# Four reorderings in a fused attention and ternary-FFN kernel: row statistics stored ahead of token transposes, two weight turns and a column sum moved, output-weight splits gathered in one place

## The reference

```python
xn = (x - mean(x)) / sqrt(var(x) + 1e-5)
q, k, v = rope(xn @ Wq.T), rope(xn @ Wk.T), xn @ Wv.T
s = softmax(causal(q @ k.T / sqrt(32))) @ v @ Wo.T
def bitlinear(x, w):                    # w: sign(round(w / (mean|w| + eps))) * mean|w|
    return absmax_clip(layer_norm(x)) @ ternary(w).T
g = silu(bitlinear(gelu(bitlinear(xn, w_fc)), w_proj))   # 512 -> 2048 -> 512
out = x + s * g
```

## Time and profile before

| | |
|---|---|
| runs | 1117.98, 1117.86, 1116.13 us; median 1117.86 |
| the profiled execution | 1117.98 us; its span in the trace 1116.3 us |
| mean granted TensorE clock | 0.997 |
| PE busy (matmul) | 1087.4 us, 97% |
| DVE, ACT, POOL busy | 865.5 us (78%), 771.7 us (69%), 519.8 us (47%) |
| PE's waits from 290 us to the end | none listed |

### The profile page before, as it was taken

The page is one execution under the profiler, slowest core; times in us unless marked ns, Lnnn a source line. Parts: engine busy times, 40 slices in busy tenths (PEclk is TensorE's granted clock), DMA queues, the critical chain, the costliest instruction groups (busy, mean ns, idle before and its releaser), DMA issues.

```text
span 1116.3 us, 19950 instructions
## 1 busy us (share of the span) xinstructions
PE 1087.4 (97%) x7404; PEld 595.0 (53%) x7404; DVE 865.5 (78%) x1623; ACT 771.7 (69%) x1478; POOL 519.8 (47%) x915
## 2 busy tenths in 40 slices
PE   4999998999999999999999999999999999999998
PEld 3565653447544584446734475444844467444763
DVE  6986975899758987589766997579874898668964
ACT  4797983379835898269862798448982688727984
POOL 2035361374625637165352745247371663626533
PEclk9999998999999999999999999999999999999999
DMA  9494013851039202491026610493013910256101
GB/s 319 161 99 93 1 22 52 110 94 39 18 52 126 73 11 40 62 137 38 2 40 94 105 39 4 67 103 86 21 26 60 153 40 2 40 79 82 39 15 64
DMA packets 86401, 75.68 MB, mean 68 GB/s; under 512 B 43168, under 2 KB 68128, under 8 KB 85792
## 3 DMA queue, kind: packets, MB, share of 16 engines
q1 hardware_dynamic: 86304, 74.41, 37.0%
HBM read 31.98 MB, written 8.40 MB: 36 GB/s over the span
## 4 chain that ended last, share of the span: by engine, by line
PE 87%; DVE 5%; ACT 3%; DMA 2%; POOL 1%; issue 1%; SPq 1%; DVEq 0%; ACTq 0%; POOLq 0%
PE banks L450 20%; PE banks L585 19%; PE banks L630 14%; PE banks L711 7%; PE banks L692 6%; PE banks L564 6%; PE banks L467 5%; PE banks L641 4%; PE banks L571 2%; ACT banks L892 2%; PE banks L484 1%; PE banks L421 1%; DMA v_sb<-in_L_attn_Wv_dram 1%; DVE mix L1201 1%; DVE arena L1171 1%
## 5 line engine op out<-in xcount | busy, mean ns | idle before, releaser
L892 ACT ACTIVATE banks<-banks,mix,scl 128x384 f32<-128x384 f32 (+2 forms) x384 | 248.2, 649 | 21.0 <-POOL mix L1416 15.5
L1201 DVE TENSOR_REDUCE mix<-banks 128x1 f32<-128x512 f32 (+3 forms) x352 | 216.0, 637 | 27.7 <-PE banks L571 23.4
L585 PE MATMUL banks<-xT,fcT 128*128 128x512 f16 x1024 | 227.8, 379 | 2.3 <-ACT xh_buf L856 1.8
L630 PE MATMUL banks<-proj_ones,arena 128*128 128x256 f16 (+1 forms) x1536 | 213.3, 273 | 0.0
L1407 POOL TENSOR_TENSOR xh_buf<-xh_buf 128x512 f32<-128x512 f32 x120 | 152.4, 1270 | 68.0 <-ACT xh_buf L856 66.6
L915 ACT ACTIVATE arena<-banks,scl 128x1280 f32<-128x1280 f32 x128 | 162.1, 1330 | 30.1 <-PE banks L692 27.2
L450 PE MATMUL banks<-xT,qkT 128*128 128x512 f16 x768 | 170.7, 383 | 0.1
L585 PEld LDWEIGHTS banks<-xT,fcT 128*128 128x128 f16 x1024 | 98.5, 98 | 121.3 <-ACT xh_buf L856 6.0
L630 PEld LDWEIGHTS banks<-proj_ones,arena 128*128 128x128 f16 x1536 | 141.7, 97 | 35.9
L1416 POOL TENSOR_SCALAR mix<-mix,scl 128x1 f32<-128x1 f32 (+1 forms) x288 | 76.5, 266 | 174.2 <-DVE mix L1201 172.8
L1401 POOL TENSOR_TENSOR xh_buf<-xr_buf,xh_buf 128x512 f16<-128x512 f32 x32 | 37.0, 1176 | 217.0 <-ACT xh_buf L828 217.0
(11 more groups left out here) (165 smaller groups left out, 1418.2 us busy)
## 6 DMA issues: line engine op xcount, KB each, us to landing
stacks<-xh_buf SPq DMA_DIRECT2D x96, 128.0 KB, 5.2
stacks<-split_buf SPq DMA_DIRECT2D x96, 128.0 KB, 7.6
out_dram<-arena SPq DMA_DIRECT2D x32, 256.0 KB, 2.0
xr_buf<-in_L_attn_x_dram SPq DMA_DIRECT2D x7, 1024.0 KB, 11.2
resid<-in_L_attn_x_dram SPq DMA_DIRECT2D x28, 256.0 KB, 4.8
stacks<-in_L_ffn_w_fc_dram SPq DMA_DIRECT2D x1, 4096.0 KB, 26.0
arena<-in_L_ffn_w_proj_dram SPq DMA_DIRECT2D x1, 4096.0 KB, 15.3
mix<-norm_row SPq DMA_DIRECT2D x8, 256.0 KB, 4.5
```

Of the source, the lines that this page charges most:

```text
L585: mm = pe.matmul(banks[:, UP_BANKS[f % NUB], :], fcT[:, c, f * P:(f + 1) * P], xT[:, part, c, :], start=(c == 0 and part == 0), stop=(c == ...
L630: mm = pe.matmul(banks[:, DOWN_BANKS[h % 3], 0:cols.stop - cols.start], hid[:, part, f, t * P:(t + 1) * P], proj_ones[:, f, cols], start=( ...
L892: mm = nc.scalar.activation(block, block, ACT.Exp, scale=col(EXP_SCALE), bias=exp_bias[:, i, h0 + k:h0 + k + 1], accum_out=row_sum[:, i, h ...
L1201: nc.vector.tensor_reduce(row_max[:, i, h0:h0 + n], scores_of(r), AX_X, ALU.max).then_inc(max_ready, 1)
```

## The change

It has four edits. None adds or removes an instruction.

- In `TURNS_IN_UP`, unit `fu[7]` is turned behind step 2 of the up-projection instead of behind step 1.
- On SP, `store_norms(b + 1)` stands ahead of `turn_tokens(b + 1)` instead of behind it; `spread_norms(b + 1)` keeps its place behind both.
- On PE, in sequence 0, `add_magnitudes(1)` stands behind step 1, ahead of its turns, instead of behind step 0 and its turn.
- On DVE, in sequence 1, `ou[2]` and `ou[3]` are split in `out_weights()`, ahead of the rotary products, instead of behind the sums of the first pair.

```diff
-        TURNS_IN_UP = {0: fu[5:6], 1: fu[6:8], 2: fu[8:9], 3: fu[9:10], 4: fu[10:11], 5: fu[11:12],
+        TURNS_IN_UP = {0: fu[5:6], 1: fu[6:7], 2: fu[7:9], 3: fu[9:10], 4: fu[10:11], 5: fu[11:12],
...
                 if not last:
+                    store_norms(b + 1)
                     turn_tokens(b + 1)
-                    store_norms(b + 1)
                     spread_norms(b + 1)
...
                     mm.then_inc(fc_ps, 1)
+                    if first and f == 1:
+                        add_magnitudes(1)
                     for u in TURNS_IN_UP.get(f, []) if first else []:
                         turn_weights(u, u + 1)
-                    if first and f == 0:
-                        add_magnitudes(1)
...
                 dve.wait_ge(ffn_step, 7)
-                for u in ou[:2]:
+                for u in ou:
                     split_weights(u)
...
-                    for u in ou[2:] if b == 1 and pair == 0 else []:
-                        split_weights(u)
```

## The result

The changed kernel took 1122.96 us (median of 5 runs, 1120.08 to 1126.37) against 1116.47 us before (5 runs): ratio 1.0054, 95% interval 1.0035 to 1.0075. It is slower, and lies above the prediction's range. Its profiled execution happened to be the quickest of all, 1117.88 us with a span of 1116.2 us, level with the one before. So two things have to be explained: what the profile shows, and why the usual execution takes 5 us more than the one it shows. The first comes out of the rows; the second only in part.

A forecast was written before the change was run, and what follows sets the result against it. PE was taken to bound the kernel, its waits few. From the profiled 1117.98 us, -6.4 (pause) + 0.85 (unit) + 4.3 (tie) gave 1116.7, with rounding 1116.8 us; range 1111.6 to 1120.8.

The forecast's parts named there:

- The pause in sequence 1: Start of sequence 1: earlier norm stores end PE's 4.2 us wait for row maxima and the half clock behind it; -6.4 us.
- the tie: Sequences 1 to 7: a transpose's semaphore can't land before the norm stores queued ahead, so PE waits; +4.3 us, chance 0.60.
- the new wait before the third pair: Sequence 1: PE waits 1.1 us for the first pair's products, which DVE makes only after the gathered splits.
- The gathered splits: Sequence 1, DVE: splitting ou[2] and ou[3] early is alone worth 0.2 us in either direction.
- The unit in sequence 0: Up-projection, sequence 0: fu[7] turned later delays DVE's rounding and ACT's square, so PE's step 3 waits longer; +0.85 us.
- the slot: Sequence 0: DVE has four slots, so fu[11] needs fu[7] turned; its rounding starts 1.6 us later, at 72.0.
- the cover of 0.8 us: Sequence 0: 0.8 us of DVE's delay is absorbed before ACT's first square starts late.
- The stores ahead of the transposes: First V tile of sequences 1 to 7: PE waits when stores land after its slack; 0 to 1.7 us each, +4.3 us.
- PE's slack: Time from the statistics to PE's first V tile: 9.50 us in sequence 1, 9.87 us in sequence 4.
- the transposes' data are held too: Rival, sequences 1 to 7: engines hold the transposes' data until stores finish, 1.5 us more per tile; 1125.0 us, chance 0.10.

The follow-up runs named there:

- the kernels that do only this: Kernel before with norm stores ahead of the transposes only between sequences 0 and 1: 1110.77 us with output splits gathered, 1111.81 us without.
- the filler: Kernel before with the two sequence 0 edits plus 22 useless matmuls ahead of PE's wait for up-projection step 3: 1117.71 us, ratio 1.0006.
- each store twice: Kernel before with norm stores ahead of all transposes, each repeated to an unread buffer from sequence 1 on: 1139.61 us in one run.
- the one store: Kernel before with output splits gathered and the four norm stores joined into one DMA of 512 elements ahead of all transposes: 1113.71 us, ratio 0.9970.

## Why the prediction was wrong, point by point

**The pause in sequence 1: right.** -6.4 us plus 0.8 for the tie there was the forecast, -5.6; the kernels that do only this measured -6.2 us (with the gathering) and -5.6 (without). The 0.8 itself turned out between nothing (the profile with the gathering) and 0.8 (the one without, 0.5 us for the first tile and 0.3 for the second). In the profile after, the wait and the half clock behind it are gone, and the new wait before the third pair is there (0.72 against 1.1 forecast).

**The gathered splits: right within what can be told.** 0.2 us in either direction was forecast, 1.0 us between the two medians was measured, with overlapping intervals; and the 0.8 us for tiles, which only the profile without the gathering has, are no part of what the splits cost.

**The unit in sequence 0: right mechanism, mis-sized.** The step "+0.85 us" had the slot, the start of the fourth rounding (72.0, measured 72.17) and the cover of 0.8 us. It left out two things: the rounding was 0.46 us slower in its new place, which with the slot makes the wait 1.4 us longer, and behind this wait of 2.7 us the clock fell in half of the executions. The two edits together cost 2.5 us (1.0024), the filler takes 2 us of that away (1.0006).

**The stores ahead of the transposes: right mechanism, mis-sized; this is the term that failed.** "+4.3 us" was worked out from the stores' landing against PE's slack, as if the tile landed together with the last store. For the six later sequences it had 3.4 us of it, 0.57 each (3.6, redone from the landing events). By the timed runs the stores ahead cost 8.4 us there, 1.4 each. That splits as follows.

First, 6.9 us are waits in the one profile of the stores alone, at a clock of 1.00. Landing and slack were sized right; what was missing is that the tile comes 0.5 us behind the last store on average. That the near standstill of the data is what makes it later is likely, not shown. The prediction had said itself that 0.5 us in every landing moves the sum by some 2.3 us. The standstill is a part of the rival "the transposes' data are held too", which had a chance of 0.10 and put 1.5 us on top of the landing.

Second, 1.5 us are not in that profile. The runs of the stores alone lie at 1117.98 and 1118.62 us with a mean clock of 1.000, and at 1121.8 and 1122.9 with 0.996 and 0.997, so a fall of the clock belongs to the slower ones. That it comes behind one of the waits for a transpose is argued, not shown, since those runs have no trace.

The profiled execution after has 3.8 us of such waits, and its 1117.88 us would have seemed to confirm the forecast. That is luck: its stores landed after 9.4 us on average where they took 10.0 with the stores alone, and none of its three waits for a tile was followed by a fall of the clock.

**The sum.** From the single edits, in ratios: -0.0058 (sequence 1) + 0.0024 (sequence 0) + 0.0075 (stores elsewhere) = 1.0041, 4.6 us. Measured was 1.0054 (1.0035 to 1.0075). The 1.4 us between lie within the intervals; what they are stays open. So does part of the 5 us between the changed kernel's profile and its median: the clock is not all of it, for three executions with the same mean clock of 0.998 took 1117.88, 1120.08 and 1121.51 us. Landings that scatter from one execution to the next, as they do between the two profiles, would do it, but only traced executions show them. The range, 1111.6 to 1120.8, took its upper end from the tie's own scatter of the waits, in which a clock that falls had no part.

## What to carry to other kernels

A transfer that is moved up in a queue is not only early itself: what stands behind it in the queue may be reported only after its slowest writes, and what stands just ahead of it now and then as well. So compare the landing of the moved one with the slack of its neighbours, and move it only where that pays. Here one `if first` turned a loss of 0.25% into a gain of 0.5%.

A wait of PE has two prices, its length and the chance that the clock falls behind it; where waits lie at 2 to 3 us, one profile doesn't show the second. Read the granted clock of all timed runs before trusting the profiled one.

## What the runs showed of the hardware

Four DMAs of 128 elements of 4 bytes to memory, whose last landing came 9.0 to 11.4 us after the first issue in the kernel before, hold up the transposes behind them. The transposes' rate fell from 181 to 25 GB/s for 3 us, and in all 28 sequence starts of the four traces with the stores ahead everywhere (the changed kernel, the stores alone, each store twice, the one store) the first tile landed after the last landing of a store that the trace has. The semaphore of a transpose issued ahead of the stores came 9.9 us after its issue in one sequence of seven; before, the median was 3.4 us from issue to landing. The rule that the prediction weighed, in the Trainium skill's "DMA: Bandwidth & Descriptors", Queues, rings and completion order (a semaphore lands only after earlier writes of its engine), agrees with the tiles behind the stores (the first 0.17 us after the last store in sequence 2 of the changed kernel). That a transfer ahead of them was late once, and that data nearly stop, goes beyond it and is the trace's own.

The fall of the clock is not a matter of the wait's length alone: behind a wait of 2.73 us at the same step it fell in one profiled execution and not in another, behind 1.92 and 2.13 us (the stores alone) the V tile ran at full speed, and in the kernel with each store twice the V tile behind 2.55 us ran at full speed (2.75 us), while the one behind 2.01 us took 4.44.
